# Moving score products ahead of the turn of the probabilities in two attention stages

## The reference, cut to what matters

```python
q_geo, k_geo = _rope(q_geo, pos, ROPE_BASE), _rope(k_geo, pos, ROPE_BASE)
k_sem2, k_geo2, v2 = pool(k_sem), pool(k_geo), pool(v)
scores = q_sem @ k_sem2.T / sqrt(32) + q_geo @ k_geo2.T / sqrt(32)
scores = where(k_pos <= pos, scores * exp(logit_scale), NEG_INF)
out = (softmax(scores) @ v2) @ Wo
x = x + out * silu(ffn(xn))
```

## Time and profile before

| what | value |
|---|---|
| three runs | 2163.65, 2164.09, 2169.98 us; median 2164.09 |
| profiled execution | 2166.91 us, its span 2165.1 us |
| busy share, TensorE, VectorE, ScalarE, GpSimd | 85%, 58%, 37%, 41% |
| mean granted TensorE clock | 0.918 |

### The profile page before, as it was taken

The page is one execution under the profiler, slowest core; times in us unless marked ns, Lnnn a source line. Parts: engine busy times, 40 slices in busy tenths (PEclk is TensorE's granted clock), DMA queues, the critical chain, the costliest instruction groups (busy, mean ns, idle before and its releaser), DMA issues. The chain is left out here.

```text
span 2165.1 us, 34584 instructions
## 1 busy us (share of the span) xinstructions
PE 1840.9 (85%) x10272; PEld 1505.3 (70%) x10272; DVE 1260.0 (58%) x2162; ACT 796.3 (37%) x1666; POOL 888.1 (41%) x642
## 2 busy tenths in 40 slices
PE   3299999999999888888649966775999999996996
PEld 2189999999999733333327845664899999995775
DVE  5145555555555469999834532652666656655886
ACT  3132222222222144566212211442666666661211
POOL 0421212212122035644503376211777878773554
PEclk7589999999999989999769987777999999998998
DMA  5420110100100321212383033102678888875664
GB/s 209 182 101 31 38 51 29 58 29 29 58 29 30 113 98 34 73 64 97 112 295 121 16 106 108 50 0 76 234 280 280 280 283 281 284 264 191 203 203 137
DMA packets 97647, 279.17 MB, mean 129 GB/s; under 512 B 13506, under 2 KB 15136, under 8 KB 94240
## 3 DMA queue, kind: packets, MB, share of 16 engines
q1 hardware_dynamic: 80320, 228.29, 30.0%
q0 software_dynamic: 17248, 49.86, 6.9%
HBM read 210.39 MB, written 67.71 MB: 128 GB/s over the span
## 5 line engine op out<-in xcount | busy, mean ns | idle before, releaser
L626 DVE TENSOR_TENSOR rffn_h<-rffn_ps_hidden,rffn_silu 128x128 f32<-128x128 f32 x272 | 79.4, 292 | 301.5 <-ACT rffn_silu L599 301.5
L599 ACT ACTIVATE rffn_silu<-rffn_ps_hidden 128x128 f32<-128x128 f32 x272 | 75.6, 278 | 458.5 <-PE rffn_ps_hidden L674 458.5
L635 DVE TENSOR_TENSOR rffn_y<-rffn_ps_y,rffn_y 128x512 f32<-128x512 f32 x272 | 188.1, 692 | 3.0 <-PE rffn_ps_y L693 1.1
L568 POOL TENSOR_TENSOR rffn_w1l<-rffn_raw,rffn_w1h 128x768 fp32r<-128x768 f32 x32 | 59.1, 1848 | 254.5 <-ACT rffn_w1h L588 254.5
L674 PE MATMUL rffn_ps_hidden<-rffn_w0h,rffn_xsh 128*128 x544 | 156.9, 288 | 7.3 <-issue 4.6
L674 PE MATMUL rffn_ps_hidden<-rffn_w0h,rffn_xsl 128*128 x544 | 154.6, 284 | 0.0
L674 PE MATMUL rffn_ps_hidden<-rffn_w0l,rffn_xsh 128*128 x544 | 154.0, 283 | 0.0
L674 PE MATMUL rffn_ps_hidden<-rffn_w1h,rffn_xsl 128*128 x544 | 153.9, 283 | 0.0
L674 PE MATMUL rffn_ps_hidden<-rffn_w1h,rffn_xsh 128*128 x544 | 153.5, 282 | 0.0
L674 PE MATMUL rffn_ps_hidden<-rffn_w1l,rffn_xsh 128*128 x544 | 153.2, 282 | 0.0
L568 POOL TENSOR_TENSOR rffn_w0l<-rffn_raw,rffn_w0h 128x768 fp32r<-128x768 f32 x32 | 59.0, 1848 | 222.2 <-ACT rffn_w0h L588 222.2
(11 more groups left out here) (631 smaller groups left out, 5897.6 us busy)
## 6 DMA issues: line engine op xcount, KB each, us to landing
moe_raw<-in_moe_w SPq DMA_DIRECT2D x47, 769.5 KB
moe_raw<-in_moe_w SPq DMA_DIRECT2D x47, 768.0 KB, 5.4
rffn_raw<-in_ffn_w SPq DMA_DIRECT2D x16, 1536.0 KB, 6.7
ys<-moe_y SPq DMA_DIRECT2D x47, 512.0 KB
xs<-route_zero SPq DMA_DIRECT2D x17, 256.0 KB
rffn_x_in<-xs SPq DMA_DIRECT2D x17, 256.0 KB, 2.9
ys<-rffn_y SPq DMA_DIRECT2D x17, 256.0 KB, 2.0
y<-in_x SPq DMA_DIRECT2D x4, 1024.0 KB
```

Source lines behind the costliest of these rows:

```text
L568: nc.gpsimd.tensor_tensor(w[j][LO][:, cols], raw[:, cols], f32(w[j][HI][:, cols]), ALU.subtract)\
L599: nc.scalar.activation(sil[n % 2][:], hb[n % 2][:, 0:P], ACT.Silu).then_inc(s_sil, 1)
L626: nc.vector.tensor_tensor(h32[n % 2][:], hb[n % 2][:, P:GU], sil[n % 2][:], ALU.mult).then_inc(s_h32, 1)
L635: nc.vector.tensor_tensor(y[:, t, :], yb[n % 2][:], y[:, t, :], ALU.add).then_inc(s_yadd, 1)
```

## The change

Three edits, none of which adds, removes or resizes an instruction, a wait or a buffer.

- Window stage: TensorE takes scores(u+2) ahead of turn(u). VectorE starts with shift(0) and then takes inverse(u), shift(u+1), probs_low(u-1), out_low, so that the low parts of a unit come behind the shift of the unit two later. ScalarE starts with exps(0) and takes probs(u), exps(u+1), probs_high(u), out_high; against before only out_high changes its place, from behind probs(u) to behind probs_high(u).
- Attention stage: `scores` is cut in two. The mask and the folded products keep the name, the geo products with their wait for the query become `geo_scores`.
- Attention stage: TensorE takes the folded products ahead of turn_p, the geo products behind it.

```diff
--- before.py
+++ after.py
@@ -2426,14 +2426,14 @@
             def out_high(g):
                 act.wait_ge(s_av, g + 1)
                 nc.scalar.copy(oT[HI][:, 2 * g:2 * g + 2, :], sb_[:].rearrange("p (a n) -> p a n", a=2)).then_inc(s_ohi, 1)
+            exps(0)
             for u in range(2 * HKV):
-                exps(u)
-                if u:
-                    probs_high(u - 1)
                 probs(u)
+                if u + 1 < 2 * HKV:
+                    exps(u + 1)
+                probs_high(u)
                 if u >= 3 and u % 2:
                     out_high((u - 3) // 2)
-            probs_high(2 * HKV - 1)
             out_high(HKV - 1)
             for i in range(2):
                 act.wait_ge(s_o, i + 1)
@@ -2555,11 +2555,13 @@
                 dve.wait_ge(s_ohi, g + 1)
                 nc.vector.tensor_tensor(oT[LO][:, 2 * g:2 * g + 2, :], sb_[:].rearrange("p (a n) -> p a n", a=2),
                                         f32(oT[HI][:, 2 * g:2 * g + 2, :]), ALU.subtract).then_inc(s_olo, 1)
+            shift(0)
             for u in range(2 * HKV):
-                shift(u)
+                inverse(u)
+                if u + 1 < 2 * HKV:
+                    shift(u + 1)
                 if u:
                     probs_low(u - 1)
-                inverse(u)
                 if u >= 3 and u % 2:
                     out_low((u - 3) // 2)
             probs_low(2 * HKV - 1)
@@ -2682,9 +2684,9 @@
             scores(0)
             scores(1)
             for u in range(2 * HKV):
-                turn(u)
                 if u + 2 < 2 * HKV:
                     scores(u + 2)
+                turn(u)
                 if u >= 2 and u % 2 == 0:
                     attend(u // 2 - 1)
             attend(HKV - 1)
@@ -3000,6 +3002,9 @@
                     for n, (u, v) in enumerate(PASSES):
                         nc.tensor.matmul(out[:], xq[i % NX][u][:, c, :], mq[:, v, c, :],
                                          start=(i == 0 and c == 0 and n == 0), stop=False)
+
+            def geo_scores(i):
+                out = sb_[i % 2]
                 pe.wait_ge(s_qlo, i + 1)
                 for g in range(HKV):
                     for n, (u, v) in enumerate(PASSES):
@@ -3021,10 +3026,12 @@
                     geo_query(n)
                 if 0 <= n - 1 < NR:
                     turn_q(n - 1)
+                if 0 <= n - 1 < NR:
+                    scores(n - 1)
                 if 0 <= n - 2 < NR:
                     turn_p(n - 2)
                 if 0 <= n - 1 < NR:
-                    scores(n - 1)
+                    geo_scores(n - 1)
                 if 0 <= n - 2 < NR:
                     output(n - 2)
```

## The result

Over 20 runs of each kernel the changed kernel has a median of 2161.24 us beside 2168.72 us; the ratio is 0.9963, with a 95% interval of 0.9953 to 0.9974. That is 8.0 us faster (5.6 to 10.2). The forecast was 14.7 us. The kernel before, over 20 runs, is 4.6 us above the median of the three runs that the prediction had, which is one part of why 2161.24 lies outside the range (8.0 us off the 2164.1 of the forecast would be 2156.1, just inside); the other is that the gain is little more than half of the forecast, and that is what has to be explained. The profiled execution has a span of 2157.6 us, 7.5 less than before.

A forecast was written before the change was run, and what follows sets the result against it. Bound by a VectorE-ScalarE relay in window units and a loop through VectorE and TensorE in attention tiles. Window -4.5 and attention -10.2 made -14.7 us: 2164.1 to 2149.4 us, range 2145 to 2157.

The forecast's parts named there:

- Plain window unit: Window-stage unit without attend: VectorE's steps from sum to sum without the wait on ScalarE's copy, 5.12 us against 7.18.
- Unit with attend: Window-stage unit with an attend block: VectorE's out_low waits for out_high behind turn, attend and scores, 9.6 us against 10.06.
- The clock in the window stage: TensorE's clock falls in gaps after attend units; each restart costs 1.4 us, once on units 5 to 6, twice at the end.
- The half weight on the first: Half a clock-restart cost, 0.7 us, on the first window unit with attend, whose TensorE gap is only 2.4 us.
- The hole in TensorE's tile: Attention stream: TensorE's wait for VectorE's probabilities before their turn goes, with 2.6 us to spare.
- the first tile: Start of the attention stream: tile 1's geo products wait for the query's low part; shift starts 2.5 us earlier.
- The steady tile: Attention tile set by TensorE's 9.17 us plus turn, copy and low part, 2.05: 11.22 us against 11.58.
- The interval from tile 1 to 2: Attention stream, counted among 11 tiles of 11.22 us each, together 123.4 instead of 128.2.
- The last interval: Attention's last tile: no query product covers; geo products start at the query's low part, shift 2.9 us earlier.
- Rival C: Attention: GpSimd's two adds block VectorE steps with two SBUF inputs in each tile, 12.47 us a tile, 2163.2 us; 6%.
- Rivals A: Window stage: the clock stays high, giving -9.4 us there and 2144.5 us in all; 12%.
- D: Attention: the clock falls inside each tile, 13.57 us a tile, +21.1 us, 2175.3 us in all; 4%.

## Why the prediction was half right

Its direction and both new orders' mechanisms hold, and so does the window stage. In the attention stage it took TensorE's chain as all that sets a tile, and left out a second round through GpSimd; that, and a low clock at both ends of the stream, is the miss.

- **Plain window unit**, 5.12 forecast: 5.11. **Unit with attend**, 9.6 by the chain over attend, scores, half a turn and the copies: 9.55 at a granted clock of 1.00. The wait named as the one that replaces the old, VectorE at the low part of oT, is where VectorE stands; the run with out_high moved shows the cause.
- **The clock in the window stage** was put into the right units. It cost 2.0 us (11.56 less 9.55) in the second unit with attend, where 1.4 stood: the low stretch was about 4 us long, not the 2.8 that was taken from the earlier trace rows. The last section took 23.2 against 22.2. The half weight on the first was not needed in this trace, which is luck: in that of the add on VectorE, whose window stage is the same code, the first unit with attend took 11.19 us at a mean clock of 0.85. Sum -3.6 for -4.5.
- **The hole in TensorE's tile** is closed, and **the first tile** gained 2.4 us for 2.5 forecast. A trace with the attention order of before (the window edits alone) had 14.60 us there instead of 15.46, so the close hit is in part luck.
- **The steady tile is the step that failed.** The prediction wrote "VectorE needs 11.58 - 1.29 = 10.29, so it has 0.93 to spare", and kept the multiply at 0.93 "as TensorE no longer waits for it". It took the 0.24 us in it as a fixed loss. But the multiply ends 0.56 us after GpSimd's add in both kernels, and this add stands behind four gathers that start with the rotation of the tile before, which VectorE makes behind the last multiply. That is a closed round, and the rows give its length. After: from the multiply's end to GpSimd's sum of the rotation 3.26 us (2062.55 to 2065.81), from there over the gathers to the add 6.37 (2072.18), the add 1.30, and 0.56 to the end of the next multiply, 11.49 us. Before: 3.27 (2043.99 to 2047.26), 6.44 (2053.70), 1.31 and 0.55, 11.57 us. Both are the tile.

```profile
2065.81 1.28 POOL L2829 TENSOR_TENSOR att_q<-att_tt 128x512 f32<-128x512 f32 x1 [3.82 <-DVE att_tt L2940]
...
2071.86 2.18 DVE L2902 TENSOR_TENSOR att_p<-att_p,att_inv 128x512 f32<-128x512 f32 x1
...
2072.18 1.30 POOL L2834 TENSOR_TENSOR att_res<-att_res,att_x_in 128x512 f32<-128x512 f32 x1
```

```profile
2047.26 1.28 POOL L2827 TENSOR_TENSOR att_q<-att_tt 128x512 f32<-128x512 f32 x1 [3.82 <-DVE att_tt L2938]
...
2053.70 1.31 POOL L2832 TENSOR_TENSOR att_res<-att_res,att_x_in 128x512 f32<-128x512 f32 x1
...
2054.63 0.93 DVE L2900 TENSOR_TENSOR att_p<-att_p,att_inv 128x512 f32<-128x512 f32 x1
```

The change shortens nothing on this round, so the tile could fall only by the 0.1 us that the gathers took less. What VectorE no longer waited for the scores (1.29 us) it stood in the multiply instead (1.48 us held, where it was 0.24): the add's start went from 0.94 us ahead of the multiply's (2042.12 to 2043.06) to 0.31 us behind it. The trace of after shows it build up: the multiply takes 0.92, 1.77 and 2.18 us in tiles 2, 3 and 4, and the intervals in which these stand are 11.18, 11.18 and 11.45 us; as long as VectorE still has a wait ahead of the low part, the longer multiply is hidden. With the round opened, by the add ahead of the gathers or off GpSimd, the tile is the forecast one, 11.18 for 11.22. So the gathers have a part in the 11.47, as the longest stretch of the round, but only by way of the add that stands behind them.

- **The interval from tile 1 to 2.** The prediction said that one tile takes 11.58 us with 128.20 for 11 intervals, but 11 times 11.58 is 127.4: the first of them was 12.43. It forecast 11.22 for it like for the others, and put the low clock of the start at nothing there. It took 12.93, with 4.4 us of it at 0.50. In all eight traces with this attention order, repaired or not, the interval follows its mean granted clock: 11.77 and 11.78 us at 0.92, 11.97 at 0.90, 12.49 at 0.86, 12.93 and 12.94 at 0.83, 13.09 and 13.15 at 0.82.
- **The last interval**, 9.9 forecast, was 12.03: the multiply is held 1.48 us there too, and from 2134.0 on the geo products run at 0.50, which makes up the rest, about 0.7. The attention half alone, whose clock stayed at 1.00 there, has 11.33; with the add moved and the clock at 1.00 it is 9.91.
- **Rival C** was this collision, at 6%. Its two blocks were one, and its condition ("in each tile") was met. It was argued away with today's 0.24 us, although these rows say more: the multiply is held, and nothing else on the round through GpSimd has time to spare, so this round is as long as the tile. By the Trainium skill, SBUF — State Buffer, "Who interferes with whom", a VectorE instruction with two SBUF inputs contends with a GpSimd instruction that reads SBUF. The trace agrees: the multiply was held in every steady tile, 1.48 us beside an add of 1.30, and none of the three steps with an operand in PSUM was longer beside the same add.
- Rivals A and D did not come: the clock fell in the window stage's gaps as before, and in the ten steady attention tiles it stayed at 1.00.

## What to carry to other kernels

When a wait is taken out of a loop, ask not only which engine has time to spare but whether another closed round is as long as the tile. An instruction that stands held by another engine, be it for 0.24 us, is a sign of one: follow what the other engine's instruction waits for, back to the held one a tile earlier, and add it up. The 0.24 us is then no bound for the loss; the hold grows to take up what the rest of the loop gains. And in an engine's list written by hand, a copy that only the far end needs (out_high) can stand ahead of one whose input comes late: two lines moved on ScalarE were worth 9.9 us of the window stage by the traces, more than the whole change gave in both stages (7.9).

## What the hardware showed unexpectedly

The multiply starts 0.31 us *ahead* of GpSimd's add (2060.38 and 2060.69) and is held all the same: it ends 0.56 us after the add's end. In the kernel before it started 0.94 us behind it and also ended 0.56 us after its end (2043.99 and 2043.43); GpSimd's row there, beside the earlier trace rows:

```profile
2042.12 1.31 POOL L2832 TENSOR_TENSOR att_res<-att_res,att_x_in 128x512 f32<-128x512 f32 x1
```

So in these rows the start of a VectorE instruction does not say that it goes ahead of the other; the add had the better of it both times. The Trainium skill, SBUF — State Buffer, "SBUF: two separate sides", has it that whichever of two such instructions starts first has the shared port pair for its whole length; by the profile's starts it was here the other one. Whether the start in the profile comes ahead of the taking of the port was not tried.
